# Forward stage: the sums on VectorE and the differences on Pool alternate strictly

## What is computed

```python
def _L1_conv_ref(x, w1_real, w1_imag, w2_real, w2_imag):
    x_ft = jnp.fft.rfft2(x)
    top = jnp.einsum('bixy,ioxy->boxy', x_ft[:, :, :m1, :m2], w1)
    bot = jnp.einsum('bixy,ioxy->boxy', x_ft[:, :, -m1:, :m2], w2)
    out_ft = jnp.zeros((b, w1.shape[1], h, wf), dtype=top.dtype)
    out_ft = out_ft.at[:, :, :m1, :m2].set(top)
    out_ft = out_ft.at[:, :, -m1:, :m2].set(bot)
    return jnp.fft.irfft2(out_ft, s=(h, w))

x = x + _L0_conv_ref(_gn(x), ...)
x = x + _L1_conv_ref(_gn(x), ...)
```

## Time and profile before

| | |
|---|---|
| median of three runs | 2686.02 us (2683.16 to 2687.36) |
| profiled execution, its own time | 2688.57 us |
| its span | 2686.7 us |
| granted TensorE clock over the span | 0.969 |
| TensorE matmul busy | 2148.0 us, 80% |
| VectorE busy | 2080.3 us, 77% |
| ScalarE busy | 1404.0 us, 52% |
| Pool busy | 935.1 us, 35% |
| DMA, mean rate | 350 GB/s |

### The profile page before, as it was taken

The page is one execution under the profiler, slowest core; times in us unless marked ns, Lnnn a source line. Parts: engine busy times, 40 slices in busy tenths (PEclk is TensorE's granted clock), DMA queues, the critical chain, the costliest instruction groups (busy, mean ns, idle before and its releaser), DMA issues.

```text
span 2686.7 us, 34793 instructions
## 1 busy us (share of the span) xinstructions
PE 2148.0 (80%) x12978; PEld 1220.7 (45%) x12978; DVE 2080.3 (77%) x2296; ACT 1404.0 (52%) x1757; POOL 935.1 (35%) x577
## 2 busy tenths in 40 slices
PE   0000089999999999999999999987777998988795
PEld 0000035665534664353555555567674554544452
DVE  7999979999999999999988888863324665545453
ACT  1111188898889888897777777741002221212110
POOL 2000024564335553366866656631101221111121
PEclk9999999999999999999999999998988999989897
DMA  9999789999999999998876777679998999999999
GB/s 399 431 430 422 333 266 345 340 347 344 341 340 349 335 343 339 338 348 313 318 258 255 258 263 266 260 281 346 367 382 331 416 416 417 416 418 417 417 417 384
DMA packets 404589, 940.99 MB, mean 350 GB/s; under 512 B 13868, under 2 KB 309084, under 8 KB 360780
## 3 DMA queue, kind: packets, MB, share of 16 engines
q1 hardware_dynamic: 213244, 577.01, 57.5%
q0 software_dynamic: 54672, 210.67, 20.0%
q10 hardware_dynamic: 136512, 151.14, 16.0%
HBM read 653.42 MB, written 285.08 MB: 349 GB/s over the span
## 4 chain that ended last, share of the span: by engine, by line
PE 49%; DMA 15%; DVE 12%; issue 7%; ACT 3%; POOL 1%; ACTq 0%; SPq 0%; DVEq 0%; POOLq 0%
PE psum L629 21%; DMA out<-arena 8%; PE psum L1119 8%; PE psum L998 7%; PE psum L1046 4%; PE psum L1093 4%; PE psum L1010 3%; DMA arena<-L_conv_w_imag 3%; DVE arena L1264 3%; DVE arena L896 2%; DVE arena L903 2%; DMA arena<-modes_out 2%; PE psum L1109 2%; DVE arena L1284 2%; ACT arena L643 1%
## 5 line engine op out<-in xcount | busy, mean ns | idle before, releaser
L629 PE MATMUL psum<-arena 128*64 128x512 f32 x4096 | 882.7, 592 | 2.2 <-DVE arena L732 1.8
L629 PEld LDWEIGHTS psum<-arena 128*64 128x64 f32 x4096 | 447.0, 136 | 437.7 <-issue 328.9
L1119 PE MATMUL psum<-tab_irow_icol,inv_t 128*128 128x512 f32 x1024 | 491.0, 603 | 46.7 <-ACT inv_t L1250 46.5
L1434 DVE TENSOR_TENSOR arena<-arena,psum 128x1024 f32<-128x1024 f32 x256 | 312.5, 1221 | 224.1 <-PE psum L1119 221.2
L1471 POOL TENSOR_TENSOR arena<-arena 128x1024 f32<-128x1024 f32 x128 | 347.9, 2726 | 191.7 <-PE psum L998 177.4
L534 POOL COPY arena<-arena 64x2321 f32<-64x2321 f32 x126 | 349.1, 2771 | 14.8 <-PE psum L629 7.1
L675 ACT ACTIVATE arena<-arena,pcur 128x2048 f32<-128x2048 f32 x128 | 268.1, 2095 | 106.4 <-DVE arena L903 101.8
L903 DVE SCALAR_TENSOR_TENSOR arena<-arena 128x2048 f32<-128x2048 f32 x128 | 319.2, 2494 | 4.0
L896 DVE SCALAR_TENSOR_TENSOR arena<-psum,pcur,arena 128x2048 f32<-128x2048 f32 x128 | 300.5, 2347 | 27.3 <-PE psum L629 26.7
L323 DVE BATCH_NORM_STATS2 arena<-arena 128x6 f32<-128x512 f32 x512 | 305.4, 676 | 14.2 <-DMA arena<-x 14.0
L1250 ACT ACTIVATE inv_t<-psum 128x256 f32<-128x256 f32 x256 | 97.5, 384 | 418.6 <-PE psum L1109 418.6
(11 more groups left out here) (192 smaller groups left out, 1823.9 us busy)
## 6 DMA issues: line engine op xcount, KB each, us to landing
arena<-x_scratch SPq DMA_DIRECT2D x254, 1024.0 KB, 8.6
arena<-x SPq DMA_DIRECT2D x120, 1280.0 KB, 9.4
arena<-x SPq DMA_DIRECT2D x64, 2048.0 KB, 12.4
x_scratch<-arena ACTq DMA_DIRECT2D x128, 1024.0 KB, 9.1
out<-arena POOLq DMA_DIRECT2D x126, 1024.0 KB, 41.6
arena<-L_conv_w_real POOLq DMA_DIRECT2D x6, 4096.0 KB, 19.8
arena<-L_conv_w_imag POOLq DMA_DIRECT2D x6, 4096.0 KB, 28.5
arena<-x SPq DMA_DIRECT2D x8, 1152.0 KB, 7.2
```

The costliest lines, as they stand in the source:

```text
L629: last = nc.tensor.matmul(bank(k * 4 + q, 512, C, e * C), wcur[j][:, e, m * C:(m + 1) * C], taps[e][:, r0:r0 + 2, m:m + W], start=(m == 0) ...
L1119: last = nc.tensor.matmul(bank(n % 2 * 2 + a), TS[n % 2][:, a * P:(a + 1) * P], icol, start=True, stop=True)
L1434: nc.vector.tensor_tensor(xw, xw, psum[:, n % 2 * 1024:n % 2 * 1024 + 1024] .rearrange("p (a k) -> p a k", a=2), ALU.add).then_inc(added, 1)
```

## The change

In VectorE's sums_of a wait is added ahead of the sum of half h: the first h differences must be done. In Pool's loop the wait for the sum of the same half, which stood inside the branch for h below 2, now stands for every h. So sum h comes behind difference h - 1, and difference h behind sum h.

```diff
@@ -1260,6 +1260,7 @@
                         dve.wait_ge(f_loaded[t % NXF], f_loaded_by(t))
                         if h >= NE:
                             dve.wait_ge(f_row_done, 2 * (h - NE) + 2)
+                        dve.wait_ge(diff_done, h)
                         half = slice(h % 2 * CG // 2, (h % 2 + 1) * CG // 2)
                         v.tensor_tensor(ED[h % NE][0][:, :, :], XWF[t % NXF][:, 0, half, :], XWF[t % NXF][:, 1, half, :],
                                         ALU.add).then_inc(sums_done, 1)
@@ -1467,7 +1468,7 @@
                         if h < 2:
                             nc.gpsimd.tensor_tensor(ED[h][0][:, :, :], XWF[0][:, 0, half, :], XWF[0][:, 1, half, :],
                                                     ALU.add).then_inc(sums_done, 1)
-                            pool.wait_ge(sums_done, h + 1)
+                        pool.wait_ge(sums_done, h + 1)
                         nc.gpsimd.tensor_tensor(ED[h % NE][1][:, :, :], XWF[t % NXF][:, 0, half, :],
                                                 XWF[t % NXF][:, 1, half, :], ALU.subtract).then_inc(diff_done, 1)
```

## The result

The changed kernel takes 2706.39 us (median of five runs, 2703.6 to 2708.32) against 2686.73 before (2683.16 to 2692.78): a ratio of 1.0077, 95% interval 1.0064 to 1.0089, 20 us slower. I had forecast 2688 with a range to 2704. The profiled execution took 2708.32 us, its span is 2706.5 us at a granted clock of 0.976, where 2686.7 stood.

What follows compares the result with a forecast made beforehand. VectorE and Pool taking turns bound the first batch, TensorE the later batches' column steps. First batch +3.3, six batches -5.8, last batch's end +3.9 make +1.4 us on 2686.02: 2687.4, called 2688; range 2677 to 2704.

Steps and rivals of the forecast that it cites:

- The turn: Forward stage: a sum on VectorE, hand-over to Pool, a difference, hand-over back; 3.74 us, bounds 3.59 to 4.04.
- The parts that TensorE binds: Later batches, TensorE's steps 2 to 8 at 28.06 us as now, and a step with columns at 6.46.
- the 3.55: Later batches: where VectorE isn't late, a sum starts 3.55 us after TensorE's step before, behind copies out of the transposes.
- the largest term: Six later batches of the forward stage: 67.99 us each in place of 68.95, -5.8 us in all.
- The gain that it stood against: Six later batches: sums no longer stand behind a difference Pool made too early, -5.8 us.
- my 67.99: Forecast length in us of one later batch of the forward stage, where 68.95 stood.
- The first batch: Start of the forward stage: 17 turns of 3.74 us, one longer by 1.97; it ends +3.3 us later.
- The end: End of the last batch: 51.88 us in place of 47.99, with two weight loads now behind difference 126; +3.9 us.
- The lost race: Rival: Pool starts before small VectorE instructions behind a sum, which are held; +15.7 us, 2703; chance 0.18.
- Long turns: Rival: some 68 sum-and-difference turns on the path take 4.04 us each; 20 us more, 2708; chance 0.10.
- Short turns: Rival: sum-and-difference turns take 3.59 us, with hand-overs at zero; 10 us less, 2677; chance 0.12.
- no effect: Rival: the lock already makes VectorE and Pool alternate, so the waits are met when reached; 2686; chance 0.05.

## Why the prediction was wrong

**The turn was mis-sized, and that carries most of the miss.** The step that failed is "I take 0.10 for that hand-over and 0.05 back". Measured: 0.17 and 0.13, the turn 3.90 in place of 3.74. The nearest row that I had was a 0.08 us start of Pool behind VectorE; back from Pool there was none, and I took a value near the zero end, though my own upper end, 4.04, was in the text. Over 17 turns it is 2.7 us, in a batch 8 x 0.16 = 1.3 us, 7.7 in all; the sum of a batch redone with 3.90 is 28.06 + 3.55 + 3.90 + 7 x 3.90 + 6.46 = 69.3, where 69.43 was measured. The parts that TensorE binds and the number of turns were right, and the 3.55 nearly: sum 11 starts 1361.44 - 1357.68 = 3.76 us behind step 8, since column copies stand ahead of it. With the right turn the six batches are slower than before and not faster, so the sign of the largest term hung on 0.12 us a turn.

**The gain that it stood against had another reason.** "The gain is that the sums no longer stand behind a difference that Pool made too early" failed too. At full clock a batch of before takes 67.49 us, less than my 67.99, so that even turns of 3.74 would have gained nothing on it. What made 68.95 of it were the stretches in which TensorE's granted clock stood at 0.5, and I took every step at full clock without asking whether it had it. That the clock would be 1.00 in all six batches afterwards was luck for the sum: without it the six batches would have lost 11.7 us and not 2.9.

**The first batch.** The start of the second turn was missed. VectorE's timeline, against the earlier trace rows:

```profile
1253.93 0.17 DVE L1337 TENSOR_SCALAR norm_values<-norm_values 128x4 f32<-128x4 f32 x1
1254.04 1.22 DVE L1265 TENSOR_TENSOR arena<-arena 128x1024 f32<-128x1024 f32 x1
...
1257.89 1.22 DVE L1265 TENSOR_TENSOR arena<-arena 128x1024 f32<-128x1024 f32 x1
...
1263.03 1.21 DVE L1265 TENSOR_TENSOR arena<-arena 128x1024 f32<-128x1024 f32 x1
...
1264.99 1.80 DVE L1357 TENSOR_TENSOR norm_values<-norm_values 128x8 f32<-128x8 f32 x1
...
1268.64 1.21 DVE L1265 TENSOR_TENSOR arena<-arena 128x1024 f32<-128x1024 f32 x1
```

L1337 took 0.17 us, as forecast, and the first sum came at once. L1357 was held, 1.80 us, and the turn around it is 1268.64 - 1263.03 = 5.61, forecast 5.71. But the turn before it is 1263.03 - 1257.89 = 5.14 us, 1.24 more than the others: the copies waited 2.94 us for TensorE, whose rows took 3.54 us. TensorE's timeline:

```profile
1257.89 3.54 PE L998 MATMUL psum<-arena,frow_fcol_both_ident_alt 128*64 128x512 f32 x8 [0.58 <-issue]
...
1262.38 1.94 PE L998 MATMUL psum<-arena,frow_fcol_both_ident_alt 128*64 128x512 f32 x8
```

The granted clock was 0.54 in the first of them and 1.00 in the second. TensorE had waited 1.81 us for L1337 at 1254.15, after which its clock fell. The kernel before has the same there, with rows of 2.80 us at 0.68 (1257.46 to 1260.26); with waits at both ends nothing was made ahead to cover it.

**The end.** 52.58 us where 51.88 was worked out, and the mechanism was seen: the loads lie between differences 126 and 127, 5.2 us from start to start. What I left out is what the queue does behind them. The prediction asks of a moved step only how long its issue holds Pool; the 6.4 MB that it moves ran into the modes load, 4.5 us. Both runs that move the loads alone show the cause, the one that moves them forward also the size.

**The rivals.** The lost race didn't happen. The view of the small lines of the changed kernel:

```profile
L1293 DVE COPY fwd_wide<-fwd_part x8: 199/220/220, 1316.5 to 1803.7; 128x128 f32<-128x128 f32 x8
...
L1324 DVE TENSOR_TENSOR arena<-arena,ncur x8: 144/145/151, 1370.4 to 1809.9; 64x1 f32<-64x1 f32 x8
```

VectorE starts its next instruction 0.07 us before the recorded end of the sum and Pool 0.17 after it, so VectorE's small instruction gets the port. Long turns, to which I gave 0.10, is the one that came: about half the way from my turn to its 4.04, on 68 turns, +10.9 us. Short turns and no effect fell. The forecast time of 2688 missed by 18.4 us: some 10 by the turn, 1 by that 3.76, 4.5 by the late weights, 1.2 by the slow second turn, 0.7 at the end, and about 1 us is left, within the spread of the runs.

**The range.** It ended at 2704 because its upper cases were taken one at a time, and none of them had a cost outside the stage.

## What to carry to other kernels

When two engines share a port, a lock that is passed by the hardware costs less than a pair of semaphores: 3.32 us a turn against 3.90 here, with hardly an instruction held in the second. Held time in a profile is a loss only where its end is late for somebody: freeing 95 us of it cost 20, and freeing a dozen small instructions of it gained 31, 9 of them by TensorE's clock. So when waits of TensorE are moved or removed, look first at how much of a stage's time passed at a low granted clock: part of a gain or a loss may be that. Look for short instructions that are held for long with a queue behind them, and order the port around those alone, with the partner kept as far ahead as its buffers allow. And when a step is moved past a wait, follow its transfers to what is queued behind them.

## What the runs showed of the hardware

- Hand-overs by semaphore: VectorE to Pool 0.17 us from the recorded end to the recorded start, Pool to VectorE 0.13, Pool to TensorE 0.10 (1270.02 + 2.35 to 1272.47 in the changed kernel). A VectorE instruction that waits for nothing starts some 0.07 before the recorded end of its predecessor.
- Passing by the lock is quicker than end to end: 3.32 us a turn, less than the 1.23 + 2.37 = 3.60 of the two instructions alone. By that, an estimate, some 3.32 - 2.37 = 0.95 us of a sum exclude a difference.
  The Trainium skill, SBUF — State Buffer, section Summary: rules for kernel authors, has the second of two such instructions blocked until the first finishes. In these recorded durations the exclusion is shorter than that.
- Four differences without a pause and with three sums between them ran in 12.34 us; handed over in order, three turns and a difference take 3 x 3.90 + 2.37 = 14.1.
- TensorE's clock: eight row matmuls take 1.94 us at a granted clock of 1.00 and 3.59 at 0.53 (1658.63 in the kernel before). It fell in some of the places of the later batches where TensorE had idled twice for VectorE, 0.8 to 1.0 and 1.5 to 1.8 us, and in none of the six batches of the changed kernel, where no pause is over 0.95.
- A load of 896 KB on Pool's queue landed 11.4 us after its issue with 6.4 MB issued 20 us ahead of it, 19.9 with them 12 us ahead, and 24.6 with them 10 us ahead.
